# Windowed attention kernel: table rows copied ahead of the softmax division on VectorE

## The chip, the cores and the metric

The kernel runs on one core of one Trainium2 chip. The metric is the device time of one execution in microseconds (us); of several executions the median counts. The profile is one execution of its own, taken with the hardware profiler.

## What is computed

The input is `x`, 4 x 750 tokens of 192 numbers (after a first stage that mixes tokens). Five stages follow each other, each added to the residual `h`: token mixing, a linear attention, a mixture of 8 experts, an attention with relative positions, and a second mixture of experts. The change lies in the fourth, whose reference is, with N = 750 tokens, 12 heads and 64 numbers per head:

```python
q = (x @ wq).reshape(B, N, H, HD).transpose(0, 2, 1, 3)
k = (x @ wk).reshape(B, N, H, HD).transpose(0, 2, 1, 3)
v = (x @ wv).reshape(B, N, H, HD).transpose(0, 2, 1, 3)
attn = jnp.einsum('bhid,bhjd->bhij', q, k) * scale
rpk = rel_pos_embed(N, rk_v, rk_h)
attn = attn + jnp.einsum('bhid,ijd->bhij', q, rpk) * scale
attn = jax.nn.softmax(attn, axis=-1)
out = jnp.einsum('bhij,bhjd->bhid', attn, v)
rpv = rel_pos_embed(N, rv_v, rv_h)
out = out + jnp.einsum('bhij,ijd->bhid', attn, rpv)
out = out.transpose(0, 2, 1, 3).reshape(B, N, H * HD)
return out @ wproj + bproj
```

`rel_pos_embed` picks for every pair of tokens a row of a vertical and a row of a horizontal table, by the distance of the two on a grid that is 27 wide.

## The kernel before

`window_attention` handles the four batches (`B`) one after the other, and each batch in two halves of `HG` = 6 heads. The four engines and the DMA queue of SyncE each have a program of their own, written out by hand in the order in which it shall run; counting semaphores (`sg[...]`, read with `wait(name, k)`) tie them together. An engine executes its list in order, so a wait stops what stands behind it.

A half has two parts. In `words`, 36 words (6 heads times 6 chunks of 125 keys) are scored, exponentiated and multiplied with the values. Between two halves lies a boundary, and the change touches only that. There are eight boundaries: seven with an old half and a new one, and the last, behind the fourth batch, with an old half alone. At a boundary these things happen:

- `value_tables` (old half). TensorE multiplies the sums of the weights with the value tables (L2041 to L2066). ScalarE copies the vertical part into `outs` (L2369), VectorE adds the horizontal part to it (L2610). Then VectorE divides: it waits for `s_db`, the count of the DMAs that bring the inverse sums into `rdb`, and multiplies each of the three head pairs of `outs` with it (L2615), which counts `out_divided`. `rdb` is no memory of its own but lies in the first three heads of `qhi`, the rounded queries.
- `query_tables` (new half). TensorE multiplies the queries with the query tables, in seven sets (`NTS`), into the four PSUM banks `t_banks`, in turn (L2091, L2097, L2098). Each set counts `table_product`. From the fifth set on, a bank has to be free first: `bank_free(m)` waits for `table_rows_act` and `table_rows_dve` to have reached m - 3.
- `relative_rows` (new half). Each set is copied out of its bank into the rows 64 and up of `work`: the even heads by ScalarE (L2381), the odd ones by VectorE (L2670, through the lambda in VectorE's `boundary`). Each of them waits for `table_product` set by set, and counts `table_rows_act` or `table_rows_dve`.
- `boundary`. On TensorE `token_values(0)` and `(1)` (L2130, the new half's values) wait for the rows of the fifth and the sixth set on both engines (`5 + c`). `project_out(0)` (L2146, the old half's output projection of one chunk of tokens) waits for `out_divided`. Then come `project_out(1)` and `first_rows(0)` and `(1)` (L2104, the new half's row scores, on which the row maxima are taken), then the remaining chunks in turn. ScalarE's `boundary` writes the rows of `qhi` (L2392), after all rows of the tables and, since `rdb` lies there, after `out_divided`; in turn with it, it rounds the values into `vhi` (L2395). VectorE goes on with `update(0)` (L2667, which adds the projected chunk to `h`), `values_rest(0)` (L2638) and `first_maxima` (L2622).

The lines of the places that the text speaks of, on TensorE and on ScalarE:

```python
if c < 2:
    wait("table_rows_act", half * NTS + 5 + c)
    wait("table_rows_dve", half * NTS + 5 + c)
...
if c == 0:
    pe.wait_ge(s_wp, 32 * i + 16 * (half + 1))
    wait("out_divided", half * NPR + NPR)
```

Of the kernel before, what the change touches and what calls it, by code (L numbers as in the profile page):

```python
# [1744 lines left out]
def window_attention(nc, keep, A, h, ident, W4, room, share, Y0, s_back):  # L1745

    ctx = ExitStack()
    with ctx:
# [64 lines left out]
        def waiter(eng, i):  # L1813
            def wait(name, k):
                eng.wait_ge(sg[name], i * PER[name] + k)
            return wait
# [127 lines left out]
        def grid_columns(view, first, gs, n):  # L1944

            return view[:, :, first:first + GRID * n].rearrange("p h (n g) -> p h n g", g=GRID)[
                :, :, :, gs[0]:gs[0] + len(gs)]

        def relative_rows(eng, wait, half, par, copy, done):

            for m, (side, runs) in enumerate(TABLE_SETS):
                wait("table_product", half * NTS + m + 1)
                rows, at = (NVG + 1, RV) if side == "v" else (GRID + 1, RH)
                dst = work[at:at + rows, par::2, :]
                for z, (gs, n) in enumerate(runs):
                    src = t_banks[m % 4][64 * z + 32 * par:64 * z + 32 * par + rows, 0:len(gs) * NPR * n]
                    if side == "v":
                        last = copy(grid_rows(dst, 0, gs, n), src.rearrange("p (g h n) -> p h g n", h=NPR, n=n))
                    else:
                        last = copy(grid_columns(dst, 0, gs, n), src.rearrange("p (g h n) -> p h n g", h=NPR, n=n))  # L1960
                last.then_inc(sg[done], 1)
            m = NTS - 1
            wait("table_product", half * NTS + m + 1)
            copy(work[RV:RV + NVG + 1, par::2, L - 1], t_banks[m % 4][32 * par:32 * par + NVG + 1, 0:NPR])
            copy(work[RH:RH + GRID + 1, par::2, L - 1], t_banks[m % 4][32 * par:32 * par + GRID + 1, NPR:2 * NPR]
                 ).then_inc(sg[done], 1)
# [538 lines left out]
        def _(dve):  # L2505
# [94 lines left out]
            def value_tables(i, half):  # L2600

                wait = waiter(dve, i)
                wait("rel_product", half * NSET + 1)
                v.tensor_copy(outs[:, :, 0], r_banks[0][:, 0:NPR]).then_inc(sg["rel_h_added"], 1)
                wait("rel_v_copied", (half + 1) * NV)
                for m, (gs, n) in enumerate(H_SETS):
                    wait("rel_product", half * NSET + 1 + NV + m + 1)
                    k = len(gs)
                    dst = grid_columns(outs, 1, gs, n)
                    v.tensor_tensor(dst, dst, r_banks[(1 + NV + m) % 4][:, 0:k * NPR * n].rearrange(  # L2610
                        "p (g h n) -> p h n g", h=NPR, n=n), ALU.add).then_inc(sg["rel_h_added"], 1)
                wait("rel_h_added", (half + 1) * (NHS + 1))
                dve.wait_ge(s_db, (2 * i + half + 1) * (32 * NPR))
                for pr in range(NPR):
                    v.tensor_tensor(outs[:, pr, 0:L], outs[:, pr, 0:L], rdb[:, pr, :], ALU.mult  # L2615
                                    ).then_inc(sg["out_divided"], 1)

            def maxima(i, u, c, bank):

                wait = waiter(dve, i)  # L2620
                wait("row_scores", u * CH + c + 1)
                v.tensor_reduce(nmx[:, u % 2, c:c + 1], bank[0:P, :, 0:376], AX.XY, ALU.max,  # L2622
                                negate=True).then_inc(sg["max_ready"], 1)

            def to_row(i, u):

                waiter(dve, i)("max_turned", u + 1)
                v.tensor_copy(mrow[:, u % 2, :], psM[0:CH, 0, 384:384 + P]).then_inc(sg["max_row"], 1)

            def boundary(old, new):  # L2630

                def values_rest(c):

                    if new is None:
                        return
                    i, half = new
                    waiter(dve, i)("vhi_ready", half * CH + c + 1)
                    v.tensor_tensor(vlo[:, c, :, :],  # L2638
                                    psS[1][0:P, c % 2, 0:HG * HD].rearrange("p (h d) -> p h d", d=HD),
                                    vhi[:, c, :, 0:64].bitcast(F32), ALU.subtract).then_inc(sg["vlo_ready"], 1)  # L2640

                def first_maxima(x):

                    if new is None:
                        return
                    i, half = new
                    maxima(i, half * HG + x // CH, x % CH, (psS[0], psM)[x % 2])

                def first_row():

                    if new is None:
                        return
                    to_row(new[0], new[1] * HG)

                def update(c):

                    if old is None:
                        return
                    i, half = old
                    wait = waiter(dve, i)  # L2660
                    if c == 0:
                        dve.wait_ge(s_bp, i + 1)
                    wait("projected", half * CH + c + 1)
                    if half == 1:
                        wait("h_updated", c + 1)
                    hc = h[:, bass.ds(i * CH + c, 1), :].rearrange("p o e -> p (o e)")
                    v.tensor_tensor(hc, hc, psO[0:P, c % 2, 0:E], ALU.add).then_inc(sg["h_updated"], 1)  # L2667

                if new is not None:
                    relative_rows(dve, waiter(dve, new[0]), new[1], 1, lambda o, x: v.tensor_copy(o, x),  # L2670
                                  "table_rows_dve")
                update(0)
                values_rest(0)
                first_maxima(0)
                first_maxima(1)
                values_rest(1)
                update(1)
                first_maxima(2)
                first_maxima(3)
                values_rest(2)  # L2680
                update(2)
                first_maxima(4)
                first_maxima(5)
                values_rest(3)
                first_row()
                first_maxima(6)
                update(3)
                first_maxima(7)
                values_rest(4)
                update(4)  # L2690
                values_rest(5)
                update(5)
                if old is not None:
                    waiter(dve, old[0])("h_updated", (old[1] + 1) * CH)
# [51 lines left out]
            def turn(i, last_batch):  # L2746

                words(i, 0, last_batch)
                keys_part(i, 1, 4)
                inverse(i, 0, NPR - 1)  # L2750
                keys_part(i, 1, 5)
                value_tables(i, 0)
                boundary((i, 0), (i, 1))
                words(i, 1, last_batch)
                if last_batch:
                    inverse(i, 1, NPR - 1)
                    value_tables(i, 1)
                    boundary((i, 1), None)
                else:
                    add_bias(i + 1)  # L2760
                    inverse(i, 1, NPR - 1)
                    keys_part(i + 1, 0, 4)
                    keys_part(i + 1, 0, 5)
                    value_tables(i, 1)
                    boundary((i, 1), (i + 1, 0))
# [92 lines left out]
```

## Time and profile before

| what | value |
| --- | --- |
| time, median of 3 runs | 1732.97 us (1730.49 to 1739.36) |
| time of the profiled execution | 1731.92 us |
| its span, first to last instruction | 1730.2 us |
| mean granted TensorE clock | 0.932 of full speed |
| TensorE matmul busy | 1538.4 us, 89% |
| VectorE busy | 1191.7 us, 69% |
| ScalarE busy | 988.4 us, 57% |
| GpSimd busy | 337.7 us, 20% |

The table gives the share of the span in which an engine worked. TensorE is the busiest, but a share of the whole span hides where it waits; for one boundary the instructions in order of time have to be read. The granted clock is the share of full speed (1.0 is 2.4 GHz, 0.5 is 1.2 GHz) that TensorE was given.

### The profile page before, as it was taken

The numbers are of one execution on the slowest core, as the hardware profiler recorded it, in microseconds if no ns is written. First come the engines' busy times: TensorE is split into PE (matmuls) and PEld (weight loads), VectorE is DVE, ScalarE is ACT, GpSimd is POOL, SyncE is SP. The second block draws the span as 40 slices with busy tenths as digits, with TensorE's granted clock in tenths as the row PEclk, the third lists the DMA queues.
The fourth block names the chain that finished last, engine by engine and source line by source line (L and its number), as shares of the span: only waits on it lengthen the run. The fifth ranks groups of instructions, "written<-read, shape, count | busy, mean of one in ns | idle before, by whom it ended". The sixth has DMA issues, their size and how long they took to land. (4 is left out here: it accounts for less than half of the span.)

```text
span 1730.2 us, 32130 instructions
## 1 busy us (share of the span) xinstructions
PE 1538.4 (89%) x10815; PEld 1414.2 (82%) x10816; DVE 1191.7 (69%) x2251; ACT 988.4 (57%) x1779; POOL 337.7 (20%) x499
## 2 busy tenths in 40 slices
PE   5982999947999999899999999999999999747997
PEld 5861999935898889889988889998899988637996
DVE  4887555549776786785786776677777677486443
ACT  5541222226677577578577678667767857372221
POOL 5131566640000000110110010010000000004443
PEclk6895999978999999999999999999999999858999
DMA  8222111163101101101100110110110100191111
GB/s 265 69 62 68 47 58 57 56 153 107 44 19 30 44 11 38 46 11 37 39 17 11 30 45 20 29 44 20 29 44 10 38 8 11 36 331 58 60 60 28
DMA packets 61936, 94.83 MB, mean 55 GB/s; under 512 B 15644, under 2 KB 46511, under 8 KB 61422
## 3 DMA queue, kind: packets, MB, share of 16 engines
q1 hardware_dynamic: 52606, 72.92, 14.3%
q0 software_dynamic: 9200, 20.21, 4.0%
q8 instruction: 78, 1.28, 0.3%
q14 instruction: 52, 0.43, 0.1%
HBM read 72.58 MB, written 21.06 MB: 54 GB/s over the span
## 5 line engine op out<-in xcount | busy, mean ns | idle before, releaser
L2622 DVE TENSOR_REDUCE a_nmx<-a_M 125x1 f32<-125x752 f32 x256 | 240.7, 940 | 134.2 <-PE a_M L2104 133.5
L2454 ACT ACTIVATE a_Phi<-a_S 125x756 fp32r<-125x756 f32 x288 | 231.1, 802 | 155.7 <-PE a_O L2227 146.0
L2730 DVE TENSOR_TENSOR a_Plo<-a_PT,a_Phi 125x756 fp32r<-125x756 f32 x288 | 280.9, 975 | 53.8 <-ACT a_PT L2454 53.0
L1924 POOL TENSOR_TENSOR a_qlo<-a_work,a_qhi 127x750 fp32r<-127x750 f32 x48 | 79.1, 1656 | 995.9 <-PE a_S L2208 508.8
L2454 ACT ACTIVATE a_PT<-a_S 125x756 f32<-125x756 f32 x288 | 229.8, 798 | 0.0
L1140 PE MATMUL m_psG<-m_w,m_xT 128*128 x788 | 167.7, 352 | 4.8 <-DVE m_xT L1331 4.7
L2208 PE MATMUL a_S<-a_qhi,a_khi 128*125 128x378 f32 x576 | 155.1, 350 | 12.6 <-issue 5.5
L2220 PE MATMUL a_O<-a_Phi,a_vhi 125*128 125x378 f32 x576 | 150.1, 342 | 1.4 <-ACT a_PT L2454 1.4
L2227 PE MATMUL a_O<-a_Plo,a_vhi 125*128 125x378 f32 x576 | 147.4, 337 | 1.0 <-DVE a_Plo L2730 0.9
L2208 PE MATMUL a_S<-a_qlo,a_khi 128*125 128x378 f32 x576 | 146.9, 336 | 0.0
L2208 PE MATMUL a_S<-a_qhi,a_klo 128*125 128x378 f32 x576 | 146.9, 336 | 0.0
L2223 PE MATMUL a_O<-a_Phi,a_vlo 125*64 125x378 f32 x576 | 146.4, 336 | 0.0
L1140 PEld LDWEIGHTS m_psG<-m_w,m_xT 128*128 128x128 f32 x788 | 136.9, 192 | 10.2 <-issue 7.7
L2104 PE MATMUL a_M<-a_khi,a_qhi 127*125 127x376 f32 x512 | 132.0, 339 | 0.4 <-DVE a_nmx L2622 0.4
L1201 PE MATMUL m_psY<-m_w,m_hidT 128*128 x696 | 130.0, 330 | 2.6 <-DVE m_hidT L1541 2.6
L1201 PEld LDWEIGHTS m_psY<-m_w,m_hidT 128*128 128x128 f32 x696 | 114.3, 189 | 9.4 <-issue 9.4
L2208 PEld LDWEIGHTS a_S<-a_qhi,a_khi 128*125 128x125 f32 x576 | 98.3, 187 | 26.1 <-issue 14.0
L2227 PEld LDWEIGHTS a_O<-a_Plo,a_vhi 125*128 125x128 f32 x576 | 104.0, 189 | 14.5 <-DVE a_Plo L2730 4.3
L1285 ACT ACTIVATE m_xT<-m_psX 128x128 fp32r<-128x128 f32 x85 | 23.6, 278 | 157.3 <-PE m_psX L1130 157.3
L2220 PEld LDWEIGHTS a_O<-a_Phi,a_vhi 125*128 125x128 f32 x576 | 101.9, 190 | 11.1 <-issue 8.0
L2208 PEld LDWEIGHTS a_S<-a_qhi,a_klo 128*125 128x125 f32 x576 | 103.9, 187 | 0.0
L2208 PEld LDWEIGHTS a_S<-a_qlo,a_khi 128*125 128x125 f32 x576 | 103.7, 187 | 0.0
(430 smaller groups left out, 2955.3 us busy)
## 6 DMA issues: line engine op xcount, KB each, us to landing
a_qhi<-a_rdens SPq DMA_DIRECT2D x48, 187.5 KB, 3.3
m_w<-in_m_w SPq DMA_DIRECT2D x16, 384.0 KB, 7.5
a_wkv<-a_w4k SPq DMA_DIRECT2D x8, 768.0 KB, 4.8
a_wq<-a_w4q SPq DMA_DIRECT2D x8, 768.0 KB, 6.3
a_wkv<-a_w4v SPq DMA_DIRECT2D x8, 768.0 KB, 5.6
m_w<-in_m_w SPq DMA_DIRECT2D x8, 576.0 KB
m_X<-m_xn SPq DMA_DIRECT2D x8, 504.0 KB
m_w<-in_m_w SPq DMA_DIRECT2D x16, 192.0 KB, 8.3
```

Of the source, the lines that this page charges most:

```text
L1140: last = nc.tensor.matmul(psG[buf][:, g, 0:half], tokens, w1[0:rows_, bass.ds(e, 1), k, g * half:(g + 1) * half].rearrange("d o f -> d (o ...
L1201: last = nc.tensor.matmul(psY[:, 0:E], hidT[:, k * 128:(k + 1) * 128], w2[:, bass.ds(here, 1), k, :].rearrange("f o e -> f (o e)"), start= ...
L1285: nc.scalar.activation(xT[:, buf, 0, :], psX[:, 0:SLOT], ACT.Copy)
L1924: pool.tensor_tensor(qlo[0:ONE, u % HG % QLO, :], work[0:ONE, u % HG, 0:L], qhi[0:ONE, u % HG, :].bitcast(F32), ALU.subtract).then_inc(sg[ ...
L2104: last = nc.tensor.matmul(bank[0:P, a, 0:376], qhi[0:ONE, u % HG, c * P:(c + 1) * P], khi[0:ONE, u % HG, a * 374:a * 374 + 376], start=Tru ...
L2208: last = nc.tensor.matmul(psS[wd % 2][0:P, a, 0:HP], kk[:, u % HG, at], qq[:, PART[a]:PART[a] + HP], start=(x == 0), stop=(x == 2))
L2220: nc.tensor.matmul(psO[:, a, 0:HP], vhi[:, c, u % HG, :], Phi[:, wd % 2, at[a]], start=(c == 0), stop=False)
L2223: nc.tensor.matmul(psO[0:HD, a, 0:HP], vlo[:, c, u % HG, :], Phi[:, wd % 2, at[a]], start=False, stop=False)
L2227: last = nc.tensor.matmul(psO[:, a, 0:HP], vhi[:, c, u % HG, :], Plo[:, wd % 2, at[a]], start=False, stop=(c == CH - 1))
L2454: last = nc.scalar.activation(to[:, wd % 2, :].rearrange("p (a l) -> p a l", a=2), psS[wd % 2][0:P, :, 0:HP], ACT.Exp, scale=SCALE)
L2622: v.tensor_reduce(nmx[:, u % 2, c:c + 1], bank[0:P, :, 0:376], AX.XY, ALU.max, negate=True).then_inc(sg["max_ready"], 1)
L2730: v.tensor_tensor(Plo[:, wd % 2, :], PT[:, wd % 2, :], Phi[:, wd % 2, :].bitcast(F32), ALU.subtract).then_inc(sg["exp_rest"], 1)
```

## The change

In VectorE's program the division of the old half's sums is taken out of `value_tables` and made a function of its own, `divide`. `boundary` calls it behind the copies of the new half's table rows and ahead of `update(0)`. Nothing is added or left out, no other engine's program changes.

```diff
                 wait("rel_h_added", (half + 1) * (NHS + 1))
+
+            def divide(i, half):
+
                 dve.wait_ge(s_db, (2 * i + half + 1) * (32 * NPR))
                 for pr in range(NPR):
                     v.tensor_tensor(outs[:, pr, 0:L], outs[:, pr, 0:L], rdb[:, pr, :], ALU.mult
...
                 if new is not None:
                     relative_rows(dve, waiter(dve, new[0]), new[1], 1, lambda o, x: v.tensor_copy(o, x),
                                   "table_rows_dve")
+                if old is not None:
+                    divide(*old)
                 update(0)
                 values_rest(0)
                 first_maxima(0)
```

VectorE's order before, at the boundary inside a batch, from the last addition to `outs` to the first copies (ISA and REGISTER_ALU are waits and counters; `a_outs<-a_outs,a_qhi` is the division, `a_work<-a_S` and `a_work<-a_M` are the copies of table rows):

```order
L2610 TENSOR_TENSOR a_outs<-a_outs,a_O 128x3x27
L1815 ISA
L2613 ISA
L2615 TENSOR_TENSOR a_outs<-a_outs,a_qhi 128x750 x3
L1815 REGISTER_ALU
L2670 COPY a_work<-a_S 29x3x162 x2
```

The division stands directly behind the additions, ahead of the first set's copies. The same engine and place in the changed kernel:

```order
L2610 TENSOR_TENSOR a_outs<-a_outs,a_O 128x3x27
L1815 ISA
L1815 REGISTER_ALU
L2673 COPY a_work<-a_S 29x3x162 x2
```

The first copies, with their wait for the first table product, now follow the additions. And the end of the copies in the changed kernel:

```order
L2673 COPY a_work<-a_S 28x3x27x4
L2673 COPY a_work<-a_S 28x3x27x3
L1815 REGISTER_ALU
L2673 COPY a_work<-a_M 29x3
L2673 COPY a_work<-a_M 28x3
L2616 ISA
L2618 TENSOR_TENSOR a_outs<-a_outs,a_qhi 128x750 x3
L2665 REGISTER_ALU
L1815 REGISTER_ALU
L2670 ISA
L2670 TENSOR_TENSOR h<-h,a_O 125x192
```

The division, with its wait for the DMAs, now stands behind the copies of the seventh set and ahead of `update(0)`. At the last boundary, which has no new half, the order is as it was.

## Rows read from the trace of the kernel before

**Rows 1.** First lines of the page: busy time of each engine.
```profile
PE 1538.4 (89%) x10815; PEld 1414.2 (82%) x10816; DVE 1191.7 (69%) x2251; ACT 988.4 (57%) x1779; POOL 337.7 (20%) x499
```
**Rows 2.** Waits of TensorE, 400 to 1510 us: waiter, released by, total us, times, longest.
```profile
PE a_S L2130 <- DVE a_work L2670: 7.3, 7, 1.5
PE a_S L2091 <- DVE a_work L2670: 6.0, 4, 3.5
```
**Rows 3.** Groups of VectorE by form: busy, mean ns | idle before.
```profile
L2615 DVE TENSOR_TENSOR a_outs<-a_outs,a_qhi 128x750 f32<-128x750 f32 x24 | 21.1, 935 | 0.9
L2670 DVE COPY a_work<-a_S 28x324 f32<-28x324 f32 x8 | 3.9, 492 | 0.2
```
**Rows 4.** TensorE in order of time, second boundary: start, us, what [idle before].
```profile
683.82 1.91 PE L2091 MATMUL a_S<-a_pairs,a_rqv 128*64 128x81 f32 x48
...
688.97 2.84 PE L2091 MATMUL a_S<-a_pairs,a_rqh 128*64 128x84 f32 x30 [0.84 <-DVE a_work L2670]
...
693.49 2.08 PE L2130 MATMUL a_S<-a_wkv,a_hn 128*125 128x384 f32 x10 [1.51 <-DVE a_work L2670]
695.40 2.11 PE L2146 MATMUL a_O<-a_wp,a_outs 128*125 128x192 f32 x12
697.22 0.65 PE L2104 MATMUL a_S<-a_khi,a_qhi 127*125 127x376 f32 x2
```
**Rows 5.** VectorE in order of time, second boundary.
```profile
684.80 2.64 DVE L2615 TENSOR_TENSOR a_outs<-a_outs,a_qhi 128x750 f32<-128x750 f32 x3
687.48 2.72 DVE L2670 COPY a_work<-a_S 29x486 f32<-29x486 f32 x4
...
694.33 0.33 DVE L2670 COPY a_work<-a_M 29x3 f32<-29x3 f32 x2
```
**Rows 6.** The last boundary, VectorE and TensorE in order of time.
```profile
1497.05 2.64 DVE L2615 TENSOR_TENSOR a_outs<-a_outs,a_qhi 128x750 f32<-128x750 f32 x3
```
```profile
1499.84 8.46 PE L2146 MATMUL a_O<-a_wp,a_outs 128*125 128x192 f32 x36 [3.60 <-DVE a_outs L2615]
```
**Rows 7.** Fourth boundary in order of time: ScalarE, then TensorE.
```profile
968.55 0.89 ACT L2381 ACTIVATE a_work<-a_S 28x324 f32<-28x324 f32 x2 [0.27 <-PE a_S L2091]
...
970.47 0.83 ACT L2392 ACTIVATE a_qhi<-a_work 127x750 fp32r<-127x750 f32 x1 [0.66 <-ACT a_work L2381]
```
```profile
971.04 2.11 PE L2146 MATMUL a_O<-a_wp,a_outs 128*125 128x192 f32 x12
```
**Rows 8.** The same two rows of the third, fifth and seventh boundary.
```profile
830.35 0.88 ACT L2381 ACTIVATE a_work<-a_S 28x324 f32<-28x324 f32 x2 [0.26 <-PE a_S L2091]
```
```profile
833.00 2.11 PE L2146 MATMUL a_O<-a_wp,a_outs 128*125 128x192 f32 x12
```
```profile
1105.24 0.89 ACT L2381 ACTIVATE a_work<-a_S 28x324 f32<-28x324 f32 x2 [0.27 <-PE a_S L2091]
```
```profile
1107.74 2.11 PE L2146 MATMUL a_O<-a_wp,a_outs 128*125 128x192 f32 x12
```
```profile
1376.32 0.89 ACT L2381 ACTIVATE a_work<-a_S 28x324 f32<-28x324 f32 x2 [0.27 <-PE a_S L2091]
```
```profile
1379.22 2.11 PE L2146 MATMUL a_O<-a_wp,a_outs 128*125 128x192 f32 x12
```
**Rows 9.** First boundary in order of time: VectorE, then TensorE.
```profile
545.52 2.64 DVE L2615 TENSOR_TENSOR a_outs<-a_outs,a_qhi 128x750 f32<-128x750 f32 x3
```
```profile
554.21 2.39 PE L2130 MATMUL a_S<-a_wkv,a_hn 128*125 128x384 f32 x10 [1.51 <-DVE a_work L2670]
556.39 3.49 PE L2146 MATMUL a_O<-a_wp,a_outs 128*125 128x192 f32 x12
559.58 0.64 PE L2104 MATMUL a_S<-a_khi,a_qhi 127*125 127x376 f32 x2
```
**Rows 10.** Busy us by stretch (PE, PEld, DVE, ACT, POOL), granted clock, DMA share, GB/s.
```profile
557.00:560.00 3.00, 3.00 (x13) 3.00 (x13) 0.82 (x2) 1.84 (x4) 2.98 (x2) 0.64 0.00 0
684.00:690.00 6.00, 5.16 (x94) 4.83 (x94) 5.78 (x9) 5.45 (x10) 0.00 (x0) 1.00 0.01 3
960.00:966.00 6.00, 6.00 (x84) 5.99 (x83) 5.75 (x10) 3.57 (x8) 0.00 (x0) 0.55 0.01 3
```

## Prediction

> **What bounds the kernel now.** I read the busy shares first: TensorE's matmuls fill 89% of the span and VectorE 69% [rows 1]. So the attention runs at TensorE's pace, and VectorE counts only where TensorE waits for it. The list of TensorE's waits says where: the values' product L2130 waited for VectorE's table rows seven times, 7.3 us in all, and the table product L2091 four times, 6.0 us, of which 3.5 belong to the start of the stage, which the change leaves alone [rows 2]. That is what the change could win: at most 7.3 + 2.5 = 9.8 us, if nothing came in its place. What would come is the next thing on TensorE's list, the output projection L2146, which needs the division. So I read each of the seven changed boundaries in order of time and asked one question: when does L2146 start, before and after? Behind it TensorE and VectorE alternate as before, so that its shift is the shift of all that follows.
>
> **Two kinds of boundary.** In the second one (684 us) TensorE has its full clock [rows 10] and VectorE is late: it divides for 2.64 us, then copies rows for 694.66 - 687.48 = 7.18 us without a hole [rows 5]. TensorE waits 0.84 us for a free bank and 1.51 us ahead of L2130, and comes to L2146 at 695.40 [rows 4]. The sixth boundary (1234 us) repeats these rows. The first (545 us) does too up to the wait of 1.51 us, only that the clock falls behind it to 0.64 over 557 to 560 us [rows 10], and the projection starts at 556.39 [rows 9]. In the fourth boundary (960 us) the granted clock is 0.55 while the tables are multiplied [rows 10], most of the stretch at the lower of the two levels, 1.2 GHz. There TensorE is the late one: ScalarE sits idle 0.27 us for the sixth table product and can copy it only at 968.55, and the projection starts at 971.04 [rows 7]. The third, fifth and seventh boundary are of this kind [rows 8]. Here VectorE has the time to divide while it would otherwise wait for products: the division is covered.
>
> **The change, step by step.** It removes nothing. Per boundary three instructions of 935 ns [rows 3] move past 14 small copies on one queue. The count of DMAs that they wait for has been reached long before: the division's idle time is 0.9 us over all 24 instructions [rows 3]. That wait costs nothing where it was, and less where it goes. No other queue is passed.
>
> *TensorE at full clock (three boundaries).* The copies start where the division did, and take the 7.18 us. I add 0.2 us for the first product: TensorE starts it at 683.82 and needs half of 1.91 us, so it ends at 684.78, and a hand-over to another engine comes on top. This hand-over is 0.15 us where VectorE's last division ends (1497.05 + 2.64 = 1499.69) and TensorE starts (1499.84) [rows 6]. Then the division, 2.64 us and some gap, 2.67, and 0.15 for the hand-over: 0.2 + 7.18 + 2.67 + 0.15 = 10.2 us behind the old start of the division. That is 695.00 in place of 695.40, a gain of 0.4 us, and the same in the sixth. In the first, 545.52 + 10.2 = 555.72 in place of 556.39 [rows 9], 0.7 us. Both waits of TensorE [rows 4] nearly go, and one of about 1.9 us ahead of L2146 takes their place. The sum of the three is -1.5 us. The bounds are 0 (if the copies wait for products longer than I think) and -0.7 for each.
>
> *TensorE at the low clock (four boundaries).* The last copies can't start before the sixth product is there. From ScalarE's start on it, VectorE needs two copies of 0.49 us [rows 3], the two of 0.33 us together [rows 5], 0.1 us of gaps, 2.64 of division and 0.15 of hand-over: 4.2 us. That gives 834.55, 972.75, 1109.44 and 1380.52 us for L2146 in place of 833.00, 971.04, 1107.74 and 1379.22 [rows 7, 8]: later by 1.55, 1.71, 1.70 and 1.30 us, +6.3 us together. The bounds are 1.0 us for one (if copies overlap by their pipelined ends) and 2.0.
>
> *ScalarE's queries.* `qhi` also waits for the division now. At 960 its start goes from 970.47 [rows 7] to about 972.8. The cover is the projection of two chunks, 1.8 us from L2146 to L2104 [rows 4]: the first query row is ready at 973.6, TensorE asks at 974.6. Cost nothing; if the cover were gone, the few tenths by which it is late. GpSimd's low parts of the queries follow from `qhi` and are needed only when the words begin, behind the whole boundary.
>
> The sum is -1.5 + 6.3 = **+4.8 us**. The profiled execution took 1731.92 us, 1.05 below the median of the runs, 1732.97; on the median it makes 1737.8.
>
> Here a rule of the Trainium skill weighs against the change. In the low-clock boundaries ScalarE, which doesn't divide, stands idle between products [rows 7]; VectorE used to fill such holes with the division, and now the division queues behind the copies' waits. The Trainium skill (TensorE: Matmul & The Clock Gate, section on the array's 16 sub-arrays) says that VectorE's queue is strictly first-in, first-out. By that rule the +6.3 us stands; were the queue free to take a ready instruction first, the low-clock boundaries would cost 0 and the sum would be -1.5 us.
>
> **The rivals.**
>
> *All boundaries at full clock.* Which boundary meets the low clock may change from execution to execution, and the change shifts when each part runs. For it: the same program met it in the tables four times out of seven. With none of them low, the gain is 7 x 0.4 = 2.8 us, 1730.2. More than that (VectorE fully off the path, up to 9.8 us, 1723) would need L2146 not to wait, against which 10.2 us of copies and division stand.
>
> *The low clock in every boundary's tables.* 7 x 1.6 = +11 us, 1744.
>
> *The new wait pulls the clock down (the other side).* TensorE would idle 1.9 us in one piece directly ahead of L2146, where before it had two short pieces. In the first boundary the clock fell right behind the idle time of 1.51 us, and two chunks' projection took 559.58 - 556.39 = 3.19 us [rows 9] against 697.22 - 695.40 = 1.82 us [rows 4]: 1.4 us more. If that happens at each of seven, six are new: +8.4 on the +4.8, 1746. It decides against me from three such falls on: 4.8 + 3 x 1.4 = 9 us. Against it: the same 1.51 us did nothing at 684 and 1234. The Trainium skill (TensorE: Matmul & The Clock Gate, section on why this matters) also ties a fall of the clock to idle gaps between bursts of matmuls, and asks for longer ones than those here; by it this rival would not come.
>
> *The change does nothing.* The order of the built program shows the move at all seven boundaries, so only equal cover could do it; two kinds that cancel are part of the forecast.
>
> **How the numbers follow.** A measurement of this kernel can tell about 0.5%, 8.7 us, from no change: below 1724.3 is faster, above 1741.6 slower. The forecast, a mix of the two kinds (two to five boundaries low, -1 to +7 us), has 0.66; all at full clock 0.12; both are no change. Low clock in all tables 0.06 and the falls behind the new wait 0.12 are slower. 0.02 stay for an unforeseen gain (faster) and 0.02 for no effect at all (no change). The range reaches from all at full clock, 1730, to the low-clock rival and a little more, 1745.
>
> **What would show it.** In the profile after: L2670's copies (now L2673) start where the division did; L2091 no longer waits for VectorE in the sets behind the start; L2130's waits for table rows shrink from 7.3 us to below 2; and L2146 waits for the division at all seven boundaries, some 1.9 us each, with the one at the end unchanged at 3.6. The steps are wrong if L2146 starts more than 0.7 us earlier at a boundary with full clock, or not later at one with the low clock; the sum is wrong if the number of low-clock boundaries differs, at about 2 us for each.

## The result, and the profile after

The changed kernel takes **1745.63 us** (median of 6 runs, 1740.49 to 1747.58) against 1733.23 us (median of 6, 1730.49 to 1739.36). The ratio is 1.0066, 95% interval 1.0052 to 1.0081: slower by 12 us, more than the 0.5% that a measurement can tell. The forecast was 1737.8 and no change; the measured median lies just above the range's end of 1745.0 (1744.4 if the ratio is put on the 1732.97 us from which the forecast started, at its edge either way). The profiled execution took 1746.66 us, its span is 1744.8, 14.6 more than before.

The page's busy line of the changed kernel answers to [rows 1]:

```profile
PE 1550.5 (89%) x10815; PEld 1425.0 (82%) x10816; DVE 1191.8 (68%) x2251; ACT 988.8 (57%) x1779; POOL 337.2 (19%) x499
```

VectorE and ScalarE are busy as long as before. TensorE executes the same matmuls and is busy for 12.1 us more, of the 14.6 by which the span grew: it did not only wait longer, its own work took longer. TensorE's waits in the attention (400 to 1525 us), as waiter, releaser, total us, times, longest:

```profile
PE a_O L2146 <- DVE a_outs L2618: 16.5, 8, 3.6
...
PE a_S L2091 <- DVE a_work L2673: 3.4, 1, 3.4
...
PE a_S L2130 <- DVE a_work L2673: 1.3, 1, 1.3
```

The waits of [rows 2] are gone at the seven boundaries; what is left of them belongs to the stage's start. In their place stands L2146's wait for the division: 16.5 less the 3.6 of the last boundary, 12.9 us, 1.84 at each. The second boundary, which ran at the full clock before [rows 4, 5], on VectorE:

```profile
687.56 1.34 DVE L2673 COPY a_work<-a_S 29x486 f32<-29x486 f32 x2 [1.21 <-PE a_S L2091]
689.18 1.34 DVE L2673 COPY a_work<-a_S 29x486 f32<-29x486 f32 x2 [0.28 <-PE a_S L2091]
690.55 0.65 DVE L2673 COPY a_work<-a_M 29x243 f32<-29x243 f32 x2
691.89 1.38 DVE L2673 COPY a_work<-a_M 28x504 f32<-28x504 f32 x2 [0.69 <-PE a_M L2091]
693.30 1.03 DVE L2673 COPY a_work<-a_S 28x336 f32<-28x336 f32 x2
694.49 0.92 DVE L2673 COPY a_work<-a_S 28x324 f32<-28x324 f32 x2 [0.15 <-PE a_S L2091]
695.44 0.33 DVE L2673 COPY a_work<-a_M 29x3 f32<-29x3 f32 x2
695.80 2.64 DVE L2618 TENSOR_TENSOR a_outs<-a_outs,a_qhi 128x750 f32<-128x750 f32 x3
```

The holes of 1.21, 0.28, 0.69 and 0.15 us come with slow table products, for this boundary now ran at the low clock. In the kernel before a division in front fills such holes (in its fourth boundary the copies ran from 963.13 to 970.32 us without one). Now the division comes behind them. TensorE in the second boundary, and in the fourth:

```profile
685.62 3.51 PE L2091 MATMUL a_S<-a_pairs,a_rqv 128*64 128x81 f32 x48
...
698.50 2.21 PE L2146 MATMUL a_O<-a_wp,a_outs 128*125 128x192 f32 x12 [1.83 <-DVE a_outs L2618]
700.42 0.64 PE L2104 MATMUL a_S<-a_khi,a_qhi 127*125 127x376 f32 x2
```

```profile
975.74 3.64 PE L2146 MATMUL a_O<-a_wp,a_outs 128*125 128x192 f32 x12 [1.83 <-DVE a_outs L2618]
978.92 1.03 PE L2104 MATMUL a_S<-a_khi,a_qhi 127*125 127x376 f32 x2
```

The first two sets of table products take 3.51 us, 1.91 before [rows 4]. In the fourth boundary, behind the wait, two chunks' projection takes 978.92 - 975.74 = 3.18 us, 1.8 before. The granted clock says why (columns as in [rows 10]):

```profile
682.00:690.00 8.00, 8.00 (x128) 7.83 (x125) 4.69 (x10) 5.70 (x9) 0.00 (x0) 0.57 0.06 23
976.00:980.00 4.00, 4.00 (x16) 4.00 (x16) 0.83 (x3) 2.74 (x5) 3.28 (x2) 0.57 0.00 0
993.00:997.00 4.00, 3.85 (x13) 3.86 (x14) 0.00 (x0) 2.78 (x3) 0.00 (x0) 0.57 0.04 10
```

I cut both traces at four places of each of the seven boundaries and added up the parts. A is from the first value-table product (L2041) to the first query-table product (L2091), B from there to the projection (L2146), C from there to the first row scores (L2104), D from there to the next L2041, which is the words. "Low" is the time at 1.2 GHz from 530 us to the end of D, from the granted clock in stretches of 1 us (its loss against full, doubled). The second profile of each comes from the experiments below.

| kernel | A | B | C | D | low |
| --- | --- | --- | --- | --- | --- |
| before | 62.4 | 80.9 | 14.1 | 792.6 | 27 |
| before, second profile | 60.5 | 81.3 | 13.9 | 794.3 | 17 |
| after | 64.1 | 87.3 | 17.6 | 794.7 | 48 |
| after, second profile | 62.6 | 86.4 | 19.5 | 795.7 | 48 |

The differences of the first profiles, 1.7 + 6.4 + 3.5 + 2.1, and 1.0 us by which the first boundary began later, make 14.7, the span's 14.6 within rounding. On the means of both pairs they are 1.9, 5.8, 4.5 and 1.8 us, 14.0 in all. For A and D that is no more than the two profiles of the kernel before differ by (1.9 and 1.7 us), so that only B and C are clear of it.

### The profile page after: what moved, and what is told of

Read it like the earlier page. It is cut to its first block and busy times, and to the rows that moved or that the text cites. A ratio compares the mean times of both kernels' runs of the same rounds, so it can differ in the third digit from the quotient of the medians.

```text
span 1744.8 us, 32130 instructions
## 1 busy us (share of the span) xinstructions
PE 1550.5 (89%) x10815; PEld 1425.0 (82%) x10816; DVE 1191.8 (68%) x2251; ACT 988.8 (57%) x1779; POOL 337.2 (19%) x499
## 5 line engine op out<-in xcount | busy, mean ns | idle before, releaser
L2104 PE MATMUL a_M<-a_khi,a_qhi 127*125 127x376 f32 x512 | 132.2, 339 | 0.5 <-DVE a_nmx L2625 0.5
```

The costliest lines, as they stand in the source:

```text
L2104: last = nc.tensor.matmul(bank[0:P, a, 0:376], qhi[0:ONE, u % HG, c * P:(c + 1) * P], khi[0:ONE, u % HG, a * 374:a * 374 + 376], start=Tru ...
```

## The experiments

Two theories went in. The **cover theory** says where the division costs time: nothing where VectorE would wait for a product anyway, its own time behind the last copy. The **theory of the falls** says that TensorE's idle time right ahead of the projection brings the low clock in the work behind it (a fall, told from C: a projection is called stretched when C is over 2 us); its rival is that the clock went low by chance, or for another reason. Medians are compared through the ratio to the kernel before on the same chip.

| kernel | us | kernel before | ratio (95% interval) | A | B | C | D | low |
| --- | --- | --- | --- | --- | --- | --- | --- | --- |
| e1, spread | 1724.94 | 1731.78 | 0.9965 (0.9952 to 0.9978) | 62.1 | 76.4 | 13.0 | 792.6 | 20 |
| e2, one late | 1727.66 | 1731.78 | 0.9974 (0.9965 to 0.9983) | 61.5 | 77.5 | 13.4 | 793.9 | 31 |
| e3, keep busy | 1732.55 | 1731.78 | 1.0004 (0.9992 to 1.0016) | 60.5 | 84.2 | 13.4 | 792.7 | 17 |
| e4, stand-in | 1758.92 | 1731.78 | 1.0158 (1.0143 to 1.0172) | 63.0 | 95.9 | 15.6 | 794.8 | 37 |
| e5, half busy | 1735.91 | 1732.85 | 1.0013 (0.9998 to 1.0028) | 63.3 | 87.0 | 13.4 | 792.5 | 31 |
| e6, spread and busy | 1728.81 | 1732.85 | 0.9980 (0.9970 to 0.9990) | 61.4 | 79.3 | 12.8 | 793.9 | 24 |
| e7, after again | 1744.30 | 1732.85 | 1.0066 (1.0044 to 1.0088) | 62.6 | 86.4 | 19.5 | 795.7 | 48 |
| e9, idle ahead | 1757.94 | 1735.81 | 1.0127 (1.0111 to 1.0144) | 64.4 | 95.0 | 16.6 | 795.7 | 48 |
| e10, idle filled | 1753.33 | 1735.81 | 1.0093 (1.0073 to 1.0113) | 64.4 | 96.6 | 13.3 | 792.5 | 37 |

**e1: the divisions spread over the copies.** Against the changed kernel:

```diff
+                def ahead(m):
+                    if old is not None and m in {0: [0], 3: [1], 6: [2]}:
+                        divide(*old, {0: [0], 3: [1], 6: [2]}[m])
...
                     relative_rows(dve, waiter(dve, new[0]), new[1], 1, lambda o, x: v.tensor_copy(o, x),
-                                  "table_rows_dve")
-                if old is not None:
+                                  "table_rows_dve", ahead)
+                elif old is not None:
                     divide(*old)
```

> Each of the three divisions goes where VectorE's copies leave a hole: the first ahead of the first set, the second ahead of the fourth, the third behind the sixth. Cover theory (a division costs nothing where VectorE would wait for a product, and its own time where it stands behind the last copy): the output projection starts 10.9 us behind the first table product at a boundary with the full clock (before 11.6 to 11.9, after 11.0) and some 11.2 at one with the low clock in the tables (before 11.45, after 12.2 to 12.95). Time: 3 us below the kernel before, 1730. Rival, that any wait of TensorE directly ahead of the projection brings low clock into the words: as often low as in the changed kernel, 1735 to 1738.

It is faster than both kernels: 1724.94 us, 0.35% less than before, where 1730 was expected. B is 76.4 us, 10.83 to 11.08 at every boundary. VectorE in its second boundary:

```profile
683.95 0.94 DVE L2621 TENSOR_TENSOR a_outs<-a_outs,a_qhi 128x750 f32<-128x750 f32 x1
684.93 2.72 DVE L2680 COPY a_work<-a_S 29x486 f32<-29x486 f32 x4
687.68 0.65 DVE L2680 COPY a_work<-a_M 29x243 f32<-29x243 f32 x2
688.36 0.94 DVE L2621 TENSOR_TENSOR a_outs<-a_outs,a_qhi 128x750 f32<-128x750 f32 x1
689.33 1.38 DVE L2680 COPY a_work<-a_M 28x504 f32<-28x504 f32 x2
690.74 1.99 DVE L2680 COPY a_work<-a_S 28x336 f32<-28x336 f32 x4
692.76 0.94 DVE L2621 TENSOR_TENSOR a_outs<-a_outs,a_qhi 128x750 f32<-128x750 f32 x1
```

There are no holes left, and the last division lies beside the values' products of TensorE (its own rows):

```profile
691.92 2.07 PE L2132 MATMUL a_S<-a_wkv,a_hn 128*125 128x384 f32 x10 [1.85 <-DVE a_work L2680]
693.83 2.15 PE L2148 MATMUL a_O<-a_wp,a_outs 128*125 128x192 f32 x12
```

TensorE still waits 1.85 us in one piece here, but ahead of the values' products. It does so at the first two boundaries alone (at the others, whose tables ran at the low clock, 0.2 to 0.5 us), and the low clock did not follow at either. Two places are few, and e10 below shows a fall behind such a wait. The rival as I put it, any wait directly ahead of the projection, has nothing to act on.

**e2: one division of three late.** Against the changed kernel, the first two are called ahead of the copies (`divide` takes the head pairs as an argument, as in e1):

```diff
+                if old is not None and new is not None:
+                    divide(*old, range(2))
                 if new is not None:
                     relative_rows(dve, waiter(dve, new[0]), new[1], 1, lambda o, x: v.tensor_copy(o, x),
                                   "table_rows_dve")
                 if old is not None:
-                    divide(*old)
+                    divide(*old, range(NPR) if new is None else range(2, NPR))
```

> One part of the change alone: two divisions stay ahead of the copies, only the third goes behind them. Cover theory: projection 11.1 us behind the first table product at the full clock, 11.4 at the low clock, so the time is that of the kernel before or 1 to 2 us less, 1732. Were each moved division to cost its share of the 12.4 us, one third of it: 1737.

1727.66 us, 0.26% less than before and less than the 1732 expected. A third of the change does not cost a third of 12.4 us but wins 4. The cost of the change is not the order as such; it begins where more division goes late than the values' products cover: TensorE waits only 0.13 us ahead of the projection at six of the seven boundaries, 0.22 at the last of them.

**e3: unread products in the wait.** Against the changed kernel, on TensorE:

```diff
                 token_values(0)
                 token_values(1)
+                if old is not None and new is not None:
+                    waiter(pe, old[0])("rel_h_added", (old[1] + 1) * (NHS + 1))
+                    for x in range(8):
+                        nc.tensor.matmul(psO[0:P, x % 2, 0:HG * HD], hn[:, 0, x % 6 * P:(x % 6 + 1) * P],
+                                         wkv[:, 0, :], start=True, stop=True)
                 project_out(0)
```

> The changed kernel with eight matrix products of 384 columns, whose results nobody reads, between the second values product and the projection, at the seven boundaries. They fill TensorE's wait of 1.83 us. Theory of the falls (the wait of TensorE ahead of the projection pulls the clock down, which gave the low stretches at 976, 993, 1379 and 1392 us): those stretches go, 1740. Rival, that the low stretches don't hang on this wait: they stay as many, 1745 to 1746.

56 matmuls more, and the kernel is 13 us faster than the changed one by the medians, 11 us by the ratios, and level with the kernel before. Its second boundary on TensorE:

```profile
693.14 1.56 PE L2174 MATMUL a_O<-a_wkv,a_hn 128*125 128x384 f32 x8
695.13 2.21 PE L2146 MATMUL a_O<-a_wp,a_outs 128*125 128x192 f32 x12 [0.42 <-DVE a_outs L2623]
697.05 0.64 PE L2104 MATMUL a_S<-a_khi,a_qhi 127*125 127x376 f32 x2
```

No projection is stretched: C is 1.92 us six times and 1.89 once, 13.4 us in place of 17.6 and 19.5. D falls to 792.7. Time at the low clock falls from 48 to 17 us, and what is left lies in the tables, in five of seven boundaries. It gave back more than expected (1740): A and B are 2.9 and 2.6 us shorter as well than the mean of the changed kernel's two profiles. These are the low stretches in the tables, which the expectation had left as they were. That the unread products shortened them is not shown: e5 below has four of them in place of eight, and its A and B are those of the changed kernel.

**e4: a stand-in for the late division.** Against the kernel before:

```diff
                     v.tensor_tensor(outs[:, pr, 0:L], outs[:, pr, 0:L], rdb[:, pr, :], ALU.mult
-                                    ).then_inc(sg["out_divided"], 1)
+                                    ).then_inc(sg["out_early"], 1)
...
                                   "table_rows_dve")
+                if old is not None:
+                    waiter(dve, old[0])("out_early", (old[1] + 1) * NPR)
+                    for pr in range(NPR):
+                        v.tensor_tensor(turning[32 * pr:32 * pr + 32, 0:L], outs[0:32, pr, 0:L], outs[0:32, pr, 0:L], ALU.mult
+                                        ).then_inc(sg["out_divided"], 1)
                 update(0)
```

> The kernel before, its division in place, and behind the copies three products of the same length on VectorE (their result is not used), for which TensorE and ScalarE wait in the division's stead. Cover theory: at a boundary with the low clock the projection starts as late as in the changed kernel, 12.2 to 12.95 us behind the first table product, although VectorE does 2.7 us more; at one with the full clock 13.5 in place of 11.0. Time 7 x 1.6 = 11 us and 2.7 for the last boundary above the kernel before, plus what the clock takes: 1747 to 1752. Rival, that the cost lies in the division's work and not its place: 7 x 2.7 us more than the kernel before and nothing hidden, 1754 and up.

The time, 1758.92 us, lies above the cover theory's number and in the rival's. The fourth boundary shows what I had wrong:

```profile
965.97 2.64 DVE L2616 TENSOR_TENSOR a_outs<-a_outs,a_qhi 128x750 f32<-128x750 f32 x3
968.64 2.72 DVE L2671 COPY a_work<-a_S 29x486 f32<-29x486 f32 x4
...
975.50 0.33 DVE L2671 COPY a_work<-a_M 29x3 f32<-29x3 f32 x2
975.86 2.86 DVE L2676 TENSOR_TENSOR a_turning<-a_outs 32x750 f32<-32x750 f32 x3
```

B is 13.64 to 13.79 at each of the seven boundaries, whatever the clock: with the division in front, VectorE works without a hole, so the stand-in adds the same 2.2 us at either clock (B was 11.45 and 11.59 before); the rest of its 2.86 us lies beside the values' products. I had expected 12.2 to 12.95 at the low clock. The size of the cover follows from it. Without a division in front B is 12.95 at a boundary whose tables ran wholly at the low clock, with one 13.66, and the stand-in is 0.2 us longer than a division. So the division in front costs 0.5 of its 2.7 us there and 2.2 are covered; at the full clock, 11.03 against 13.79, it costs 2.5. So the theory's place for the cost holds and my number for this run did not.

**e5: half of the unread products.** The edit is e3's with `range(4)`.

> The changed kernel with four unread products in TensorE's wait ahead of the projection in place of eight: some 1.1 us of the 1.83 us stay idle. If the idle time there is what brings the low clock, and shorter ones bring less of it: between the kernel with eight (1732.6) and the one with none (1745.6), 1735 to 1740. If any work there is enough: 1733. If it was no effect of the wait but of the order of runs: 1745.

1735.91 us, between the two, nearer to e3. C is 13.4 us: four products are enough to end the falls right behind the wait. A and B are as long as in the changed kernel. The first boundary says how much of them is chance. Up to its products this kernel's program is that of the changed kernel and of e3, which ran the first tables at the full clock (B 11.03). Here the granted clock was 0.50 over 545 to 551 us, with TensorE busy all the time, and B is 12.96. This profile was of a run (1738.17 us) above the median of its own, so the tables' part may be worse in it than usual.

**e6: e1 with six unread products ahead of the values' products.**

```diff
+                if old is not None and new is not None:
+                    waiter(pe, old[0])("rel_h_added", (old[1] + 1) * (NHS + 1))
+                    for x in range(6):
+                        nc.tensor.matmul(psO[0:P, x % 2, 0:HG * HD], hn[:, 0, x % 6 * P:(x % 6 + 1) * P],
+                                         hn[:, 0, 0:HG * HD], start=True, stop=True)
                 token_values(0)
                 token_values(1)
```

> The spread divisions with six unread products in TensorE's wait of 1.85 us ahead of the values product. If that wait too brings low clock to the next tables: 1720 to 1723, with fewer low stretches than the five of the spread kernel. If a wait ahead of the values product is harmless, and only one right ahead of the projection is not: 1725, or 1 to 2 us more where the tables ran at the low clock and the products have no wait to lie in.

0.9980 against e1's 0.9965: no gain, B is 2.9 us longer, and the tables meet the low clock as often, at five boundaries. Since e1 had a long wait ahead of the values' products at two boundaries only, the run says that filling it does not pay, not that such a wait is harmless.

The low stretches early in the words (part D) are not shown to belong to the new wait. The one at 993 us of the changed kernel stands behind another wait of TensorE, ahead of the words' first product, and e2, with 0.13 us of wait ahead of the projection, shows the same (the changed kernel, then e2):

```profile
993.15 0.77 PE L2208 MATMUL a_S<-a_qhi,a_khi 128*125 128x378 f32 x2 [1.84 <-issue]
```

```profile
708.96 0.61 PE L2208 MATMUL a_S<-a_qhi,a_khi 128*125 128x378 f32 x2 [1.85 <-issue]
711.00:714.00 3.00, 3.00 (x11) 3.00 (x11) 1.49 (x2) 2.38 (x4) 0.00 (x0) 0.51 0.01 3
```

e6 has one too, behind 1.90 us. The kernel before waits there as well (1.52 and 1.54 us, no fall). In e3 and e5 waits of 1.78 and 1.81 us at this place were followed by none.

**e7 and e8: a second profile of the two kernels.**

> The changed kernel once more, for a second profile. The theory that the wait ahead of the projection brings low clock: again low stretches of over 6 us in at least four of the seven boundaries' tables and some right behind the projection's start; 1740 to 1748. The rival, that the first profile met them by chance: three or fewer, none behind the projection.

> The kernel before once more, for a second profile: three to five boundaries with low clock in the tables, 20 to 27 us of low clock between 530 and 1480 us (the first profile has 27), 1729 to 1736.

The changed kernel again took 1744.30 us, and spent the same 48 us at the low clock. Projections were stretched (C over 2.7 us) in five boundaries, in three in the first profile. Two of its falls:

```profile
836.00:840.00 4.00, 4.00 (x17) 4.00 (x16) 1.15 (x3) 2.60 (x5) 3.29 (x2) 0.57 0.00 0
1256.00:1260.00 4.00, 4.00 (x16) 4.00 (x15) 0.88 (x3) 2.69 (x5) 3.28 (x2) 0.57 0.00 0
```

Long stretches in the tables (over 6 us) came only twice, where four were expected, so their number changes between executions; the falls do not go away. (The first boundary had one in the kernel before too, behind 1.51 us of wait ahead of the values' products.) The kernel before (1732.54 us) had one stretched projection, the first boundary's, as in its first profile, and tables at the low clock in three boundaries rather than four, 17 us in all where 20 to 27 were expected.

**e9 and e10: idle time without a late division.** e9 is e1 with one wait ahead of `project_out(0)`; e10 has nine of e3's products in front of it.

```diff
                 token_values(1)
+                if old is not None and new is not None:
+                    waiter(pe, new[0])("qhi_ready", new[1] * HG + 2)
                 project_out(0)
```

> The kernel with the spread divisions, and TensorE waits for the second row of queries ahead of the projection at the seven boundaries, which is there some 2.1 us later than the projection used to start. Theory of the falls (idle time right ahead of the projection brings the low clock behind it): 7 x 2.1 = 14.7 us for the wait itself, 1739.6, and at least three stretches of low clock between the projection and the next tables, each 1.5 us more: 1744 to 1750. Rival, that the falls have to do with the division's late place and not with TensorE's idle time: 1739 to 1741 and no such stretch.

> The same with nine unread products in front of that wait, so that the projection starts as late and TensorE is busy for 1.5 of the 2.1 us. Theory of the falls: the stretches of low clock behind the projection go, and those in the tables get fewer or shorter; 1738 to 1740, 5 to 10 us less than without the products. Rival: the same time as without them.

The wait cost more than thought: B is 18.6 us longer than in e1, 2.65 for each boundary and not 2.1. Both medians lie above what was expected, and the kernel before was at 1735.81 on this chip. What tells the theories apart is the pair. With the wait left idle, three projections are stretched (C 3.31, 2.78 and 2.84), and C and D together are 812.3 us; with it filled none is, and they are 805.8. The stretch behind the wait in e9, and the same place in e10:

```profile
846.00:850.00 4.00, 4.00 (x16) 4.00 (x17) 1.02 (x3) 0.78 (x2) 1.96 (x2) 0.62 0.00 0
```

```profile
844.00:848.00 4.00, 3.46 (x21) 3.46 (x22) 1.69 (x4) 1.42 (x3) 2.58 (x2) 1.00 0.00 0
```

e10 is 4.6 us below e9 by the medians, though the intervals of the ratios overlap at their edge and its profile is of its slowest run. The stretched projections come from TensorE's idle time ahead of them, not from where VectorE divides. Counted over the profiles of the changed kernel and its variants, with 1.8 us or more of idle time right ahead of the projection 13 of 28 were stretched (3 and 5 in the changed kernel, 2 in e4, 3 in e9), with 1.3 us or less none of 42 (e1, e2, e3, e5, e6, e10). It need not be the wait ahead of the projection, though. In e10's second boundary the wait fell ahead of the values' products, as in e1, and the clock fell there:

```profile
698.50 3.53 PE L2132 MATMUL a_S<-a_wkv,a_hn 128*125 128x384 f32 x10 [1.85 <-DVE a_work L2686]
```

```profile
700.00:704.00 4.00, 4.00 (x14) 4.00 (x13) 0.60 (x3) 3.02 (x5) 2.29 (x2) 0.50 0.00 0
```

Its projection is not stretched only because the values' and the unread products took the low clock. The expected 5 to 10 us were too many: the low clock was met between the value tables and the projection in six of e9's boundaries and in all of e10's.

## Why the prediction was right or wrong, point by point

*The view of the path* was right. The waits of [rows 2] were worth what was left of them only until the next item on TensorE's list, and that item was L2146, with 1.84 us of wait at each boundary where 1.9 was forecast. One reading was wrong: of L2130's 7.3 us, 1.3 belong to the start of the stage and stay, as the list above shows, so that the change could win at most 6.0 + 2.5 = 8.5 us and not 9.8. The forecast's sum does not use that bound.

*The full-clock boundaries.* Only the first was one. Its projection came 11.03 us behind the first table product; the working gives 11.2. The hand-over was 0.06 us (553.81 + 2.64 = 556.45, start 556.51) and not 0.15:

```profile
553.81 2.64 DVE L2618 TENSOR_TENSOR a_outs<-a_outs,a_qhi 128x750 f32<-128x750 f32 x3
```

```profile
556.51 3.88 PE L2146 MATMUL a_O<-a_wp,a_outs 128*125 128x192 f32 x12 [1.83 <-DVE a_outs L2618]
```

*The low-clock boundaries.* 12.8 to 13.15 us were forecast, 12.2 to 12.95 measured. Six of seven were of this kind in the first profile and in the second, where the forecast took four. The change's sum, +4.8 us, measured +6.4 in the first pair of profiles and +5.8 on the means (B). The number of boundaries was mis-sized, the mechanism and its price were right. So was the reading of first-in, first-out: above, VectorE stands idle for 1.21 us at 687.56 and divides only at 695.80, though the additions that it follows in the kernel before had ended ahead of that hole; and e1 changes nothing but the order on that queue. Whether the number rose from four to six by the change or by chance is open: the forecast named it as what the sum hangs on, and e5's first boundary shows that chance alone moves it.

*ScalarE's queries "cost nothing".* Nearly: C is 1.92 us where the clock did not fall, 1.82 before. The tenth goes with the wait, not with the queries: TensorE's load of `outs` as weights, which began 0.17 us ahead of the first product before (695.23 and 695.40 at the second boundary), now stands behind the wait too, as the list of those who waited for L2618 shows (engine, what, total us, times):

```profile
  PE a_O L2146: 16.5, 8
  PEld a_O L2146: 12.9, 6
```

In e9, where the division is long done and only the wait is left, C is 1.91 to 1.92 as well. That is 0.7 us in all, and no step had it.

*The step that failed* is the weight given to the rival "the new wait pulls the clock down". I gave it 0.12, since the same 1.51 us "did nothing" at two of three boundaries. Its mechanism and its price (1.4 us) came as put: 3.6, 3.2 and 3.2 us for the projection in three boundaries of the first profile, 2.8 to 3.5 in five of the second, where 1.9 is what it takes without a fall. Two of these three and four of these five are new, for the first boundary had one before. C grew by 4.5 us on the means, on top of the forecast's sum, which had nothing for it, and e3, e5, e9 and e10 show the cause. It is the largest single part of what the sum lacks. By the Trainium skill (TensorE: Matmul & The Clock Gate, section on why this matters) gaps as short as these should have left the clock alone. The traces disagree: it fell behind 1.83, 1.83 and 1.92 us of idle time in the first, fourth and seventh boundary.

The sum that the traces give is 5.8 (B) + 4.5 (C) + 1.8 (D) + 1.9 (A) = 14 us, and the medians differ by 12.4. Against the forecast's +4.8, B is 1.0 too long and C 4.5; A and D, 3.7 together, are within what two profiles of one kernel differ by. The measured time came to lie at the upper edge of the range because the range was drawn out to the rivals, not because the sum was near: it missed by 7.6 us.

*What stays open.* Whether the tables run at the low clock. The changed kernel spends 34 and 27 us there in its two profiles, the kernel before 24 and 14, e3 17. e3's shorter A and B could mean that the wait of one boundary has to do with the next one's tables, but e5, e9 and e10 do not sort by it, the first boundary ran either way under one program, and no run tells why. Open too is which waits of about 1.8 us bring a fall: ahead of the projection about half did, ahead of the values' products one in e10 and none of two in e1, ahead of the words some did and some did not. Nor is it known why e4, whose TensorE also waits about 2 us ahead of the projection, shows one stretched projection and half of another (C 3.57 and 2.44) and not three or more.

## What to carry to other kernels

A wait is worth no more than the distance to the next thing on the same engine's list, so find that item and what it needs before moving work past another. When a step can fill holes, do not choose between "ahead" and "behind": cut it into its instructions and put each where a hole is (e1: 0.35% faster than before, where the whole step moved made it 0.66% slower). And count an idle TensorE twice where its clock falls: once for the wait, once for the work behind it. One profile does not tell how often that is, for the same program met three falls and then five.

## What the runs showed of the hardware

Adding 56 unread matmuls made the changed kernel 13 us faster by the medians (e3, 1732.55 against 1745.63; by the ratios 11). Idle time of 1.83 us, with work at full clock ahead of it, was followed by a granted clock of 0.57 to 0.63 over 4 us in three to five of seven places; about 1.1 us of idle (e5) was followed by none. The clock was also low without any idle time ahead: 0.50 over 545 to 551 us in e5, with TensorE busy for all of them, where the same program ran at 1.00 in the changed kernel's profile. And behind a wait the first load of weights is not hidden: two chunks' projection takes 1.92 us in place of 1.82.
